# Preparation stage of a conditioned residual block on one core: norms of the rotation on ScalarE, a later split of the output weights, and a later load of the second stack

## The reference

```python
# x: (2, 1024, 256), D = 256, 16 heads of 16, hidden size 1024
def _normalize(q):
    return q / jnp.sqrt(jnp.sum(q * q, axis=0, keepdims=True) + 1e-8)
# layer 0: the quaternion parts of x are gated and rotated
x_filtered = ifft(fft(x_quat, axis=1) * spectral_gate, axis=1).real   # the gate is constant along the axis
x = x + hamilton(_normalize(q_left), hamilton(x_filtered, _normalize(q_right) * conj_sign))
# layer 1: attention and a gated feed-forward layer, each behind an RMS norm with conditioned scale and bias
y = _tc_rmsnorm(x, t, g1w, g1b, b1w, b1b)
x = x + softmax((y @ Wq.T) (y @ Wk.T).T / sqrt(16)) (y @ Wv.T) @ Wo.T
y = _tc_rmsnorm(x, t, g2w, g2b, b2w, b2b)
x = x + (silu(y @ gate_w.T) * (y @ hid_w.T)) @ out_w.T
```

## Time and profile before

| | |
|---|---|
| time, median of 3 runs | 546.85 us (546.74 to 547.5) |
| time of the profiled execution | 547.42 us |
| its span | 545.6 us |
| PE busy | 534.7 us (98% of the span) |
| DVE busy | 402.7 us (74%) |
| ACT busy | 378.8 us (69%) |
| POOL busy | 146.1 us (27%) |
| granted clock of TensorE | 1.0 |

### The profile page before, as it was taken

The page is one execution under the profiler, slowest core; times in us unless marked ns, Lnnn a source line. Parts: engine busy times, 40 slices in busy tenths (PEclk is TensorE's granted clock), DMA queues, the critical chain, the costliest instruction groups (busy, mean ns, idle before and its releaser), DMA issues.

```text
span 545.6 us, 10880 instructions
## 1 busy us (share of the span) xinstructions
PE 534.7 (98%) x4274; PEld 300.5 (55%) x4274; DVE 402.7 (74%) x446; ACT 378.8 (69%) x746; POOL 146.1 (27%) x156
## 2 busy tenths in 40 slices
PE   8899999999999999999999999999999999999997
PEld 8777653333333333333333333334278889888886
DVE  4986679999999999999999999993626454321212
ACT  3646769999999998999999999997953333322222
POOL 4214720211303302001100001300726364443322
PEclk9999999999999999999999999999999999999999
DMA  6169575220651562442343341110110010010101
GB/s 215 64 201 167 196 206 66 71 72 16 125 111 54 116 109 59 79 68 69 70 67 73 63 72 43 32 43 13 32 41 0 11 40 0 2 40 0 40 0 40
DMA packets 24163, 37.96 MB, mean 70 GB/s; under 512 B 9192, under 2 KB 11368, under 8 KB 24104
## 3 DMA queue, kind: packets, MB, share of 16 engines
q1 hardware_dynamic: 22816, 32.55, 25.7%
q10 hardware_dynamic: 1296, 4.72, 3.3%
HBM read 21.97 MB, written 14.94 MB: 68 GB/s over the span
## 4 chain that ended last, share of the span: by engine, by line
PE 91%; DVE 3%; ACT 3%; DMA 2%; issue 1%; POOL 0%; SPq 0%; DVEq 0%; POOLq 0%; ACTq 0%
PE psum L1238 31%; PE psum L1255 28%; PE psum L1370 25%; ACT prob L903 2%; PE psum L1352 1%; DMA scr_qk<-qk_parts 1%; PE psum L1408 1%; PE psum L1394 1%; PE psum L1309 1%; PE psum L1215 1%; DVE xs L1025 1%; DVE nmax L1044 1%; DMA q_st<-nmax_t 1%; DVE x L1034 0%; PE psum L1442 0%
## 5 line engine op out<-in xcount | busy, mean ns | idle before, releaser
L1044 DVE TENSOR_REDUCE nmax<-psum 128x1 f32<-128x1024 f32 x256 | 310.3, 1221 | 21.0 <-PE psum L1255 20.6
L903 ACT ACTIVATE prob<-psum 128x512 f32<-128x512 f32 x512 | 276.7, 601 | 30.3 <-PE psum L1352 6.9
L1352 PE MATMUL psum<-q_st,k_st 50*128 50x512 f32 x512 | 179.5, 444 | 0.4 <-DMA q_st<-nmax_t 0.2
L1255 PE MATMUL psum<-k_st,q_st 48*128 48x512 f32 x512 | 178.9, 444 | 0.8 <-DVE nmax L1044 0.6
L1370 PE MATMUL psum<-prob,v_sb 128*17 128x256 f32 (+1 forms) x1960 | 158.1, 394 | 2.6 <-ACT prob L903 0.8
L1255 PEld LDWEIGHTS psum<-k_st,q_st 48*128 48x128 f32 x512 | 72.5, 184 | 102.8 <-DVE nmax L1044 75.6
L1370 PEld LDWEIGHTS psum<-prob,v_sb 128*17 128x17 f32 x1960 | 33.3, 95 | 89.1 <-ACT prob L903 80.2
L1352 PEld LDWEIGHTS psum<-q_st,k_st 50*128 50x128 f32 x512 | 72.8, 184 | 7.6 <-ACT prob L903 6.8
L1199 DVE TENSOR_TENSOR h_f<-psum,silu_g 128x512 f32<-128x512 f32 x32 | 22.1, 692 | 70.8 <-PE psum L1238 65.8
L939 ACT ACTIVATE silu_g<-psum 128x512 f32<-128x512 f32 x32 | 19.1, 596 | 75.6 <-PE psum L1238 75.6
L753 POOL TENSOR_TENSOR h_lo<-h_f,h_hi 128x512 fp32r<-128x512 f32 x32 | 42.1, 1315 | 75.2 <-ACT h_hi L920 75.2
(11 more groups left out here) (120 smaller groups left out, 548.5 us busy)
## 6 DMA issues: line engine op xcount, KB each, us to landing
scr_qk<-qk_parts SPq DMA_DIRECT2D x16, 512.0 KB, 3.0
q_st<-scr_qk SPq DMA_DIRECT2D x42, 128.0 KB, 4.8
k_st<-scr_qk SPq DMA_DIRECT2D x42, 128.0 KB, 5.3
scr_o<-ot SPq DMA_DIRECT2D x16, 256.0 KB
f_raw<-in_ft ACTq DMA_DIRECT2D x6, 512.0 KB, 5.9
attn<-scr_o SPq DMA_DIRECT2D x64, 32.0 KB, 1.8
sums<-scr_sum SPq DMA_DIRECT2D x64, 32.0 KB, 1.8
x_t<-in_xt SPq DMA_DIRECT2D x3, 512.0 KB, 3.3
```

The lines of the kernel that those rows point to most:

```text
L903: nc.scalar.activation(prob[(GH * s + h) % PR][:, :], e_bank("S", s, h), ACT.Exp).then_inc(e_used, 1)
L1044: nc.vector.tensor_reduce(out=nmax[:, b, e, pair, t:t + 1], in_=slot, axis=AX.XY, op=ALU.max, negate=True).then_inc(max_used, 1)
L1255: return nc.tensor.matmul(max_slot(item)[:, half, :], q_st[g % SLOTS][rows, pair, lt * P:(lt + 1) * P], k_st[g % SLOTS][rows, pair, half * ...
L1352: nc.tensor.matmul(e_bank("S", s, i), k_st[g % SLOTS][rows, pair, kt * P:(kt + 1) * P], q_st[g % SLOTS][rows, pair, half * HALF:(half + 1) ...
```

## The change

Three edits in the preparation. The squares and sums of the two quaternions move from four DVE instructions to two of ACT, the addition of epsilon to POOL, and POOL's memset of `v_sb` waits for `rot`. The weight split `("W", 1)` is left with the value weights, and the output weights become `("W", 2)` behind `("xs_T", 3)`. `load_stack(1)` moves in SP's walk from behind the save of tile (1, 1) to behind that of tile (2, 0), past `copy_ones` and four saves.

```diff
+W_PARTS = ((0, 1), (2,), (3,))
@@ order
         tail = [("SC", 2), ("L0", 3), ("SC", 3), ("QK", 0, 3), ("xs_T", 2), ("V", 1, 0), ("V", 1, 1),
-                ("QK", 1, 2), ("QK", 1, 3), ("xs_T", 3)] + [tile for tile in qkv(2) + qkv(3) if tile != LATE_TILE]
+                ("QK", 1, 2), ("QK", 1, 3), ("xs_T", 3), ("W", 2)] + [tile for tile in qkv(2) + qkv(3) if tile != LATE_TILE]
@@ SP
                     save_parts(*rest)
-                    if rest == (1, 1):
+                    if rest == (2, 0):
                         load_stack(1)
@@ POOL
-            pool.wait_ge(norms_summed, 1)
-            nc.gpsimd.tensor_tensor(small[:, 10:12], small[:, 6:8], neg_half[:, 0:2], ALU.pow).then_inc(norms_rooted, 1)
+            pool.wait_ge(norms_summed, 2)
+            nc.gpsimd.tensor_scalar(small[:, 8:10], small[:, 6:8], QEPS, None, ALU.add).then_inc(norms_guarded, 1)
+            pool.wait_ge(norms_guarded, 1)
+            nc.gpsimd.tensor_tensor(small[:, 10:12], small[:, 8:10], neg_half[:, 0:2], ALU.pow).then_inc(norms_rooted, 1)
+            pool.wait_ge(rot_ready, KT)
             nc.gpsimd.memset(v_sb[:, :, :, DH:VW], 1.0).then_inc(consts_ready, 1)
@@ POOL
-                    for i in range(2):
-                        low_weights(2 * step[1] + i)
+                    for i in W_PARTS[step[1]]:
+                        low_weights(i)
@@ ACT
+            act.wait_ge(coef_loaded, 16)
+            nc.scalar.activation(small[:, 0:4], qc[:, 0:4], ACT.Square, accum_out=small[:, 6:7]).then_inc(norms_summed, 1)
+            nc.scalar.activation(small[:, 4:6], qc[:, 4:6], ACT.Square, accum_out=small[:, 7:8]).then_inc(norms_summed, 1)
@@ ACT
-                    act.wait_ge(w_loaded[rest[0]], 16)
-                    for i in (2 * rest[0], 2 * rest[0] + 1):
+                    act.wait_ge(w_loaded[W_PARTS[rest[0]][0] // 2], 16)
+                    for i in W_PARTS[rest[0]]:
@@ DVE
-            link(nc.vector.tensor_tensor(small[:, 0:6], qc[:, 0:6], qc[:, 0:6], ALU.mult))
-            nc.vector.reduce_sum(small[:, 6:7], small[:, 0:4], AX.X)
-            link(nc.vector.reduce_sum(small[:, 7:8], small[:, 4:6], AX.X))
-            nc.vector.tensor_scalar_add(small[:, 6:8], small[:, 6:8], QEPS).then_inc(norms_summed, 1)
```

More of the change, by code:

```diff
@@ L333, in build @@
         norms_summed = sem("norms_summed")
+        norms_guarded = sem("norms_guarded")
         norms_rooted = sem("norms_rooted")
```

## The result

The changed kernel takes 552.75 us (median of 6, 551.34 to 558.14) against 547.21 for the kernel before in the same rounds: ratio 1.0109, interval 1.0087 to 1.0131, so 1.1% slower. The forecast was 551.9 us, range 548.3 to 553.8, with slower at 0.81. Its profiled execution took 552.32 us; the span is 550.5, 4.9 us more than before.

A forecast was written before the change was run, and what follows sets the result against it. PE, 91% of the span, was taken as the bound, measured at the first scores: 81.2 against 76.1 us, so 547.42 + 5.1 = 552.5, and 551.9 with the median 0.57 below; range 548.3 to 553.8.

The forecast's parts named there:

- Norms: Start of the preparation: `rot` ready about 0.5 us earlier, but PE's warm-up ends at 7.41, so PE gains 0 to 0.1.
- Output weights: DVE's scaling of chunk 1: `xs` ready 1.0 us earlier, all of it PE's gain; bounds 0 and 1.3.
- The wait at (1, 3): ACT's wait for the save of (0, 3) shrinks by 3.4 us; tile 4.4 us earlier, PE gains 0.7.
- The chain to the save of (2, 0): ACT, POOL, SP: tile (2, 0) starts at 54.4, its save is at 58.6, the 12 loads from 59.0 to 64.4 us.
- The queue: Saves behind the 12 loads wait for all of them: first lands at 75.4 to 76.8, (2, 3) at 78.4 us.
- The maxima: `load_max(0)`, behind two more saves in the same queue, lands at 81.2 us; the first scores wait for it.
- 5.1 us of delay: First scores at 81.2 against 76.1: PE loses 5.1 us, in place of a gain of 1.7.
- the shorter queue: Rival: saves overtake some loads or loads run faster; first scores 1 to 3 us late, 548 to 550 us; chance 0.15.
- The small copies: Rival: the four `copy_ones` transfers, not the loads, hold the saves; both gains stay, 545.15 us; faster had chance 0.12.
- the likeliest case: Whole kernel: slower by 3.7 to 6.8 us, likeliest time 551.9 us; chance 0.66.
- The 77.0 of the lower bound: Landing of the save of (2, 3) at its earliest: loads 12.0 us, saves at 383 GB/s, 1.3 to land; gives + 3.7.

The follow-up runs named there:

- the kernel with the copies aside: The kernel before, with the four small copies of the row of ones (`copy_ones`) moved behind the save of tile (1, 3): 547.31 us, ratio 0.9999.
- `FILL` = 24: The changed kernel with 24 products on the identity on TensorE ahead of the first scores: 550.38 us, ratio 1.0059.

## Why the prediction was right, step by step

- **Norms, 0 to 0.1 us for PE.** In the time of the edit alone nothing shows, but the reason was too narrow. I took the warm-up's end (7.41) from one execution as fixed. The same 26 instructions took 4.48 to 5.77 us over the traces, and then the second piece of `rot` is what PE waits for (0.9 us in the kernel with the copies aside, which has the old norms). In the changed kernel the first square came 0.24 us earlier. The gain is real, but in the order of before the save queue swallowed it, and in the changed order the maxima did. Nor does everything follow from the first scores, as I had assumed: with the new norms 0.6 us is gained near 218 us.
- **Output weights, 1.0 us.** Right: 3.19 to 2.18, wait 1.3 to 0.3.
- **The wait at (1, 3) goes.** Right: tile (1, 3) at 49.69, 4.7 us earlier (I had 4.4).
- **The chain to the save of (2, 0).** Part 1 of (2, 0) was done at about 58.1, the loads at 58.67 (I had 58.6 and 59.0).
- **The queue.** Right in kind. The first save behind the loads landed at 64.58 + 10.2 = 74.8 (I had 75.4 to 76.8), the one of (2, 3) at 65.56 + 11.8 = 77.4 (I had 78.4). ScalarE's tile (3, 3) started at 77.45 (I had 78.4); its long wait came one tile earlier, at (3, 2).
- **The maxima, at 81.2.** Mis-sized: the last was issued at 70.92 and landed at 79.35. One us of the 1.8 comes from the saves; the rest is that I let the maxima wait for two full saves. The save of (3, 1), issued just before them, landed at 68.67 + 11.2 = 79.9, after them. The Trainium skill (DMA: Bandwidth & Descriptors, Queues, rings and completion order) says that completion is not first in, first out for an issuing engine, and that a later transfer which uses a single DMA engine can be complete before an earlier one is on the other 15. The trace agrees that the later transfer landed first (79.35 against 79.9); how many DMA engines the maxima used isn't shown.
- **The clock.** Left out of the sum: about 2 us. My 5.1 us of delay was 1.7 too much (3.37 measured), and the clock, less the 0.6 us gained near 218 us, nearly makes up for it. That the time came within 0.9 us of 551.9 is luck: two terms off by about as much in opposite directions. With the clock kept (`FILL` = 24) the kernel takes 550.38 us, inside the range, but where I had put the shorter queue.
- **The rivals.** The small copies hold nothing. The first scores, 3.4 us late, lie between the shorter queue (1 to 3 us) and my point, and just below my lower bound for the likeliest case (+ 3.7).
- **Two sums.** The 77.0 of the lower bound does not follow from its terms: 59.0 + 12.0 + 3 x 1.4 + 1.3 is 76.5, and 77.9 with the save that stands ahead. And the ends of the range, 548.3 and 553.8, are not quite 546.85 + 1.1 = 547.95 and 546.85 + 6.8 = 553.65. Neither changes the verdict.

## What to carry to other kernels

When a batch of transfers is moved, list what is issued behind it on the same queue until its bytes are through, and ask for each who waits; here it was four transfers of 4 KB with the whole attention stage behind them. In this kernel a load that was not urgent was better cut in two and put where the queue had room: two halves gave 544.64 us where one block gave 545.9 or 552.75. A wait that idled TensorE for over 4 us had a second price behind it, in the clock, which the wait's own row doesn't show. And when two terms of a forecast are wrong in opposite directions, the total hides both: compare the terms with the trace one by one.

## What the runs showed of the hardware beyond that

- After 5.5 us without a product, TensorE's granted clock was 0.50 for 80 to 85 us; with 0.5 us idle in the same place it stayed at 1.00 there. With 3.2 us idle in the profiled one, nine of eleven executions had a mean clock below 1.0. In one trace (11 warm-up products) it fell to 0.50 at about 76 us with no gap over 0.5 us in the 6 us before.
- The same 26 warm-up instructions at the start took from 4.48 to 5.77 us in different kernels' traces, at a granted clock that the profile gives as 1.00 throughout. Why is open.
- A save of 512 KB that was queued behind 12 loads landed after four small transfers issued behind it.
